# A third PSUM place for the filter outputs, gates spread at the start, and the norm's small operations moved to GpSimd

## What is computed

```python
x = x + tanh(g_xattn) * ssm(ctx, ctx, layernorm(x), ssm_kernel, D, head_dim=8)
x = x + tanh(g_ffn)   * moe(layernorm(x), Wg, W1, W3, W2, sw1, sw3, sw2)
# ssm:  kv = outer product of the 8 rows of a head of ctx with each other
#       out = causal convolution of kv with ssm_kernel[head], plus kv * D[head]
#       out = sum over i of out[i, j] * q[i], q = layernorm(x)
# moe:  softmax router, best of 8 experts, capacity 256 tokens, plus a shared expert
```

## Time and profile before

| | |
|---|---|
| median of 3 runs | 214.48 us (214.38 to 215.14) |
| the profiled execution | 214.29 us, its span 212.6 us |
| granted TensorE clock over the span | 0.991 of full speed |
| busy: PE, DVE, ACT, POOL | 198.7, 159.9, 91.9, 123.8 us |

### The profile page before, as it was taken

One profiled execution on the slowest core, in us unless ns is written; L12 is line 12 of the kernel. 1 busy time (PEld: TensorE's weight loads), 2 busy tenths in 40 slices (PEclk: granted clock), 3 DMA queues, 4 the chain that ended last, 5 costly groups with the idle time before them and its releaser, 6 DMA issues.

```text
span 212.6 us, 4239 instructions
## 1 busy us (share of the span) xinstructions
PE 198.7 (93%) x1441; PEld 184.0 (87%) x1441; DVE 159.9 (75%) x518; ACT 91.9 (43%) x182; POOL 123.8 (58%) x129
## 2 busy tenths in 40 slices
PE   5979999899999999999999998999999999999960
PEld 5957789679998989988989998999999999999950
DVE  4798788966998987589867877776856995878530
ACT  2242733193443651322348258654373445624400
POOL 4379999274648599614583253370072687677671
PEclk9999999999999999999999999999999999999996
DMA  5799993000000010010201799845537689422221
GB/s 158 245 339 359 371 396 133 0 0 3 5 0 0 0 53 17 33 54 0 92 10 50 229 357 360 298 125 138 166 106 245 187 261 329 128 78 72 67 91 49
DMA packets 21497, 29.77 MB, mean 140 GB/s; under 512 B 2834, under 2 KB 18970, under 8 KB 21476
## 3 DMA queue, kind: packets, MB, share of 16 engines
q1 hardware_dynamic: 18964, 23.24, 33.3%
q0 software_dynamic: 2304, 6.05, 8.7%
q10 hardware_dynamic: 208, 0.22, 0.4%
HBM read 21.32 MB, written 8.45 MB: 140 GB/s over the span
## 4 chain that ended last, share of the span: by engine, by line
PE 83%; DVE 4%; DMA 4%; issue 3%; ACT 2%; POOLq 1%; ACTq 0%; SPq 0%; DVEq 0%; POOL 0%
PE fb L1294 16%; PE z L1294 14%; PE z L1206 11%; PE tp L1231 10%; PE z L1203 6%; PE z L1315 6%; PE z L1329 5%; PE fb L1329 4%; DMA x_sb<-x 3%; PE fb L1315 2%; DVE terms L509 2%; PE tp L1243 2%; PE tp L1340 2%; DMA dcol<-skip_d 1%; DVE stats L923 1%
## 5 line engine op out<-in xcount | busy, mean ns | idle before, releaser
L509 DVE TENSOR_TENSOR terms<-z,qr 128x512 f32<-128x512 f32 (+2 forms) x192 | 48.9, 326 | 6.5 <-PE z L1206 6.4
L1206 PE MATMUL z<-kv,toep 128*128 128x288 f32 x128 | 41.5, 406 | 0.0
L1294 PE MATMUL fb<-xTh,wh_gu 128*128 128x256 f32 (+1 forms) x104 | 31.9, 306 | 0.2 <-issue 0.2
L490 POOL TENSOR_TENSOR kv<-ct 128x768 f32<-128x768 f32 x15 | 27.4, 1827 | 6.6 <-PE z L1206 3.3
L1203 PEld LDWEIGHTS z<-kv,toep 128*128 128x128 f32 x128 | 22.1, 190 | 9.2 <-issue 4.8
L716 POOL DMA_INDIRECT kv<-out,tok x16 | 20.4, 1273 | 16.3 <-DMA out<-x_sb 11.7
L1203 PE MATMUL z<-kv,toep 128*128 128x144 f32 x128 | 26.8, 291 | 2.8 <-DVE terms L509 1.9
L1294 PE MATMUL fb<-xTl,wh_gu 128*128 128x256 f32 (+1 forms) x104 | 29.0, 279 | 0.0
L1294 PE MATMUL fb<-xTh,wl_gu 128*128 128x256 f32 (+1 forms) x104 | 29.0, 279 | 0.0
L662 POOL TENSOR_TENSOR terms<-terms 128x512 f32<-128x512 f32 x16 | 20.2, 1281 | 14.1 <-DVE terms L509 14.0
L667 POOL DMA_INDIRECT xd_scratch<-xrow,dest x16 | 16.7, 1044 | 17.1 <-DVE xrow L1002 7.3
(11 more groups left out here) (154 smaller groups left out, 417.9 us busy)
## 6 DMA issues: line engine op xcount, KB each, us to landing
terms<-w SPq DMA_DIRECT2D x16, 352.0 KB, 4.3
ct<-ctxt SPq DMA_DIRECT2D x3, 768.0 KB, 8.8
xd_scratch<-xrow SPq DMA_DIRECT2D x4, 516.0 KB, 9.7
kv<-xd_scratch SPq DMA_DIRECT2D x8, 258.0 KB, 3.4
out<-x_sb SPq DMA_DIRECT2D x8, 256.0 KB, 2.6
terms<-w SPq DMA_DIRECT2D x8, 256.0 KB, 4.7
x_sb<-x SPq DMA_DIRECT2D x3, 512.0 KB, 6.0
toep<-kskip_scratch SPq DMA_DIRECT2D x3, 512.0 KB, 9.8
```

The source lines that it names most:

```text
L490: eng.tensor_tensor(dst, left, right, ALU.mult)
L509: return eng.tensor_tensor(view(terms, t0 + row * TROW + col, [[64, 2], *td]), view(src, zo, [[512, 2], *zd]), view(qr, q0 + qo, [[CW, 2], ...
L1206: mm = pe.matmul(z[s % 2][:, k, 0:KVH], toep[:, h, 0:P], view(kv, o, [[1, KVH]]), start=False, stop=True, skip_group_check=True)
L1294: mm = pe.matmul(bank[0:rows(blk, c), m * 256:(m + 1) * 256], wt[w % 2][:, col:col + rows(blk, c)], xt[:, place, k, first:first + 256], st ...
```

## The change

Five edits:

- PSUM: `fb` becomes one tensor `fbz` of two banks, and the filter outputs of slots 0 to 11 rotate over three places, z[0], z[1] and fbz. From slot 12 they use the two old places. A place is waited for by the last slot that used it (`z_before`).
- Gates: their two DMAs go from SP's queue to ACT's, behind the first piece of ctx. The matmul that spreads them (in slot 6 before) comes right behind `convolve(0)`. ACT copies the result to SBUF (`gate_bc`) ahead of its squares of group 0, and takes the tanh of the copy in slot 6. PE's first use of the third place (slot 2) waits for that copy.
- Norms: L928 and L929 leave DVE. POOL makes `veps` and `mneg` at the head of `scale_and_bias`, with a wait between `veps` and what follows. DVE signals POOL behind the last L926.
- ln1 of group 3: stats in slot 13 in place of 17, POOL and ACT parts in slot 14 in place of 18. Its `turn_q` stays in slot 21. The order of the norms stays.
- `router_placed` now waits for one DMA of `small_in` in place of three.

```diff
+THREE_BANKS = 12
...
+NORM_SOONER = 4
...
     if step in PREPARING:
-        g, late = divmod(s - STEPS[step], UNITS)
-        return g + 1 if late == 0 and 0 < g + 1 < NG else -1
+        sooner = NORM_SOONER if step != "turn_q" else 0
+        return next((g for g in range(1, NG) if s == UNITS * (g - 1) + STEPS[step] - (sooner if g == NG - 1 else 0)), -1)
...
+def z_place(s):
+
+    return s % 3 if s < THREE_BANKS else (s - THREE_BANKS) % 2
+
+
+def z_before(s):
+
+    return max((k for k in range(s) if z_place(k) == z_place(s)), default=-1)
...
-        fb = [ctx.enter_context(nc.psum_tensor(f"fb{i}", [P, 512], F32)) for i in range(2)]
+        fbz = ctx.enter_context(nc.psum_tensor("fbz", [P, 2, 512], F32))
+        fb = [fbz[:, i, :] for i in range(2)]
+        z_banks = [*z, fbz]
...
-            sp.dma_start(gates[:, 0:1], bass.AP(g_x.tensor, g_x.offset, [[0, 1], [1, 1]])).then_inc(small_in, 16)
-            sp.dma_start(gates[:, 1:2], bass.AP(g_f.tensor, g_f.offset, [[0, 1], [1, 1]])).then_inc(small_in, 16)
...
+                chain(pool.tensor_scalar(veps[:, :], mv[:, :, 1], EPS, None, ALU.add))
+                pool.tensor_scalar(mneg[:, :], mv[:, :, 0], -1.0, None, ALU.mult)
                 chain(pool.tensor_tensor(rstd[:, :], veps[:, :], mhalf[:, :], ALU.pow))
...
             act.dma_start(ct[:, 0, 0:4 * CW], ctxt[0, :, 0:4 * CW]).then_inc(ctx_first, 16)
+            act.dma_start(gates[:, 0:1], bass.AP(g_x.tensor, g_x.offset, [[0, 1], [1, 1]])).then_inc(gates_in, 16)
+            act.dma_start(gates[:, 1:2], bass.AP(g_f.tensor, g_f.offset, [[0, 1], [1, 1]])).then_inc(gates_in, 16)
...
             q_copy(0)
+            act.wait_ge(spread, 2)
+            act.activation(gate_bc[:, :], fb[1][:, 2:4], ACT.Copy).then_inc(gates_copied, 1)
             for c in range(1, 4):
                 squares(0, c)
...
-                    act.wait_ge(small_in, 16 * 3)
-                    act.wait_ge(spread, 2)
-                    act.activation(tg[:, :], fb[1][:, 2:4], ACT.Tanh).then_inc(tanh_done, 1)
+                    act.wait_ge(small_in, 16)
+                    act.wait_ge(gates_copied, 1)
+                    act.activation(tg[:, :], gate_bc[:, :], ACT.Tanh).then_inc(tanh_done, 1)
...
-                chain(ins)
-                dve.tensor_scalar(veps[:, :], mv[:, :, 1], EPS, None, ALU.add)
-                dve.tensor_scalar(mneg[:, :], mv[:, :, 0], -1.0, None, ALU.mult).then_inc(stats_done, 1)
+                ins.then_inc(stats_done, 1)
...
-                if s >= 2:
-                    pe.wait_ge(prods, s - 1)
+                if z_before(s) >= 0:
+                    pe.wait_ge(prods, z_before(s) + 1)
+                elif z_place(s) == 2:
+                    pe.wait_ge(gates_copied, 1)
+                zs = z_banks[z_place(s)]
...
             convolve(0)
+            pe.wait_ge(d_in, 1)
+            pe.wait_ge(gates_in, 32)
+            pe.matmul(fb[1][:, 2:4], ones[0:1, :], gates[:, :], start=True, stop=True).then_inc(spread, 1)
             for s in range(SLOTS):
                 if 1 <= s < CONV:
                     convolve(s)
-                if s == ROUTER_SLOT:
-                    pe.wait_ge(small_in, 16 * 3)
-                    pe.matmul(fb[1][:, 2:4], ones[0:1, :], gates[:, :], start=True, stop=True).then_inc(spread, 1)
```

More of the change, by code:

```diff
@@ L278, in build @@
         tg = sb("tg", [P, 2])
+        gate_bc = sb("gate_bc", [P, 2])
         ebase = sb("ebase", [P, GB, E])
@@ L333, in build @@
         small_in = sem("small_in")
+        gates_in = sem("gates_in")
+        gates_copied = sem("gates_copied")
         shared_gu_in = sem("shared_gu_in")
@@ L947, in products @@
                     dve.wait_ge(tp_ready, TP_AT[("r", before, 1)] + 1)
-                multiply(dve, s, z[s % 2]).then_inc(prods, 1)
+                multiply(dve, s, z_banks[z_place(s)]).then_inc(prods, 1)
             def first_residual(g, k):
@@ L1201, in convolve @@
                     o = (4 * g + i) % KVRING * KVQ + h % 4 * KVH
-                    pe.matmul(view(z[s % 2], k * 512 + GB, [[PL, NPL], [1, GB]]), toep[:, h, P:2 * P],
+                    pe.matmul(view(zs, k * 512 + GB, [[PL, NPL], [1, GB]]), toep[:, h, P:2 * P],
                               view(kv, o, [[PL, NPL], [1, GB]]), start=True, stop=False,
                               skip_group_check=True)
-                    mm = pe.matmul(z[s % 2][:, k, 0:KVH], toep[:, h, 0:P], view(kv, o, [[1, KVH]]),
+                    mm = pe.matmul(zs[:, k, 0:KVH], toep[:, h, 0:P], view(kv, o, [[1, KVH]]),
                                    start=False, stop=True, skip_group_check=True)
```

## The result

The changed kernel takes 215.76 us (median of 18 runs, 214.58 to 217.47) against 214.44 us for the kernel before, timed beside it on the same chip (18 runs, 213.88 to 215.14): a ratio of 1.007, interval 1.0049 to 1.0091. That is 1.3 us slower and above the predicted range. The profiled execution took 215.43 us with a span of 213.7 us, 1.1 us more than the span of before.

A forecast was written before the change was run, and what follows sets the result against it. The prediction took PE to be bound, up to `turn_xT` of group 0, by POOL's norm chain. Three times s = 0.37 us less 1.19 us of slack gave -0.08 us, so 214.4 us, range 213.2 to 215.6.

The forecast's parts named there:

- term s: Time the two small POOL operations add to each `scale_and_bias`: 0.37 us, between 0.27 and 0.65.
- What bounds the stream: Up to `turn_xT` of group 0, PE waits for ACT, which waits for POOL's `nbias`; removed DVE waits reappear there.
- Rival B: POOL isn't the chain and PE keeps the third place's gain: 2.6 us, giving 211.9 us; chance 0.07.
- The slacks: Time that absorbs POOL's delay before `turn_xT`: 0.18 us on POOL, 0.40 and 0.27 on DVE, 0.34 on ACT.
- Steps 2 to 5: From ln1 of group 2 to ACT's q copy: s added twice more, less the slacks, leaving -0.08 us.
- rival C: POOL's operations are dear in slots 2, 10 and 11: 215.2 us at s = 0.65, 216.3 at 1.0; chance 0.10.
- Step 1: `scale_and_bias(1)` has no idle time ahead, so `nbias` and `turn_q` of slot 5 come about 0.4 us later.
- The first norm: `nbias` 0.35 us later, or 0.8 if both operations wait for DVE's L490; swallowed by `turn_q` of slot 5.
- rival D: PE's 2.2 us standstill before `turn_xT` costs its clock: +1 to +1.5 us, 215.4 to 215.9 us; chance 0.06.
- Behind it each engine follows PE, and the shift goes through to the end: After `turn_xT` of group 0 at 46.6 us, PE's gain or loss there reaches the end unchanged.
- Moved norm, gates and their DMAs: ln1 of group 3 four slots sooner worth 0 to PE; gate DMAs on ACT's queue 0; gate matmul covered by a wait.

The follow-up runs named there:

- x7: The changed kernel with POOL's two small operations done twice in every norm; 219.21 us.
- x3: The changed kernel with ln1 of group 3 back in slots 17 and 18; 215.62 us, ratio 1.0090 to the kernel before.
- x4: The kernel before with only the two small norm operations moved to POOL; ratio 1.0048 to the kernel before.
- y2: The changed kernel with 16 chained memsets at the head of POOL's program; ratio 1.0044 to the kernel before.
- x5: The kernel before with only the third place and early gates, norms on DVE and in their old slots; ratio 0.9946 to the kernel before.
- x1: The changed kernel with 16 identity transposes between `turn_q` and `turn_xT` in slot 13; 214.65 us, ratio 1.0035 to the kernel before.
- y1: The changed kernel with the small operations back on DVE and 16 chained memsets heading POOL's program; 213.66 us, ratio 0.9950 to the kernel before.
- x8: The changed kernel, unchanged, timed again on another chip; 215.68 us, ratio 1.0019 to the kernel before.

## Why the prediction was wrong

The forecast was 214.4 us, range 213.2 to 215.6; it came to 215.76. Two steps of the sum failed. The term s, the price of the small operations on POOL, was set at 0.37 us and measured 0.55 to 0.70 at the three norms, which turns -0.08 us at `turn_xT` into +0.49. And the shift was to go through to the end unchanged: the tail added 0.69 us in the trace, and the clock fell in some runs. With s alone set right the sum would still lie within the range. Point by point:

- *What bounds the stream.* Right. `turn_xT` of group 0, behind ACT, behind POOL's `nbias`; the removed waits for DVE came back as waits for ACT (0.88 us at 22.68, foretold 1.2 us at 22.5; 2.39 us at 45.87, foretold 2.2). Rival B is out: with 1.9 us of waits gone the stream was no shorter.
- *The size s*: the term that was mis-sized. Foretold 0.17 + 0.07 + 0.13 = 0.37; measured 0.23 (`veps`) + 0.09 + 0.19 (until the power starts, 19.01 to 19.20) = 0.51 us; the start behind the kv work comes 0.11 later (0.08 us behind its end, where the power of before started 0.03 ahead of it), and the power lasts 1.04 in place of 1.00 us. From K to the end of `nbias` that made 0.70 us at the first norm in the stream, and it works out at 0.64 and 0.55 us at the next two: a mean of 0.63, near the upper end of the range of s, 0.65. I took one input to be a little less dear than the two of a product (0.20); the row says 0.23 for one input and a constant.
- *The slacks* were a little larger than read. Steps 2 to 5 had 0.18 + 0.27 + 0.40 + 0.34 = 1.19 us. From the trace: 0.18, then 0.48 us at DVE's second residual (L1132 to L957 took 3.47 us before, 2.99 us after), then the 0.27 of the two operations as read (from the end of the aggregate to POOL's start 0.36 us before, 0.09 after), then 0.43 us on ACT, as the q copy starts 0.10 us before xrow ends. That is 1.36, and 0.70 + 0.64 + 0.55 - 1.36 = +0.53 us, against the +0.49 measured. With the form of the sum kept and only s set right, 0.70 + 0.64 + 0.55 - 1.19 = +0.70 us, close to rival C's lower price (+0.76), it would have said 215.2 us. So C was the case for the stream, and 0.10 was too little for it. x7 confirms the slope of three: +1.78 us for another 0.5 to 0.6.
- *Step 1*: `turn_q` of slot 5 is 0.69 us later from K on, foretold 0.4. It is s again.
- *The first norm*: `nbias` ended at 9.53 us in place of 8.88, 0.65 us later, within the foretold 0.35 to 0.8, and swallowed by slot 5 as the prediction says. DVE's statistics started 0.30 us later there (4.75 in place of 4.45 us, behind a DMA), so the change itself made 0.35. `veps` on POOL took 1.18 us beside DVE's L507 (6.61 to 7.83). The Trainium skill (SBUF — State Buffer, Who interferes with whom) says that such a pair excludes each other for a whole instruction. The trace agrees: 1.18 against 0.23 us. The rule was no reason for a different time.
- *The clock*: rival D had its mechanism and its price right (+1 to +1.5 us; measured 1.5) and the chance too low. It came on top of the rest in 7 of 18 runs; it moves the median by about 215.76 - 215.35 = 0.4 us. That the median lies in the 215.4 to 215.9 us foretold for D is luck: the runs without a low clock have 215.35 us, and most of the loss is C and the tail. The prediction held its rivals to exclude each other and so had no place for C, D and more in one kernel.
- *"Behind it each engine follows PE, and the shift goes through to the end"*: wrong. This was the step that nothing was read for. The shift arrived at the last matmul (+0.59 us from K on, 0.41 in the span's own time, 204.94 to 205.35), but the tail took 0.69 us more, by its place in POOL's program. No rival had it. Any change to the number of POOL's instructions, even in idle time, could have caused it.
- *Moved norm, gates and their DMAs*: 0, right (x3; the gates' matmul stands at 13.19 us in the wait for the Toeplitz matrices).

The account: +0.49 us in the stream, 0.10 between it and the last matmul and +0.69 in the tail make the 1.28 of the traces; the clock adds 0.4 in the median. That is 1.7 against 1.3 us measured, where K is known in the profiles alone. Other kernels fit the same prices. x4: 0.50 + 0.54, a ratio of 1.0048, measured 1.0048. y2: 0.47 + 0.0 and 3 of 12 low-clock runs at 1.5 us, a mean of 0.85, 1.004, measured 1.0044. x5: -0.94, 0.9956, measured 0.9946. x3: 0.48 + 0.62 and 3 of 6 low-clock runs, 1.0087, measured 1.0090. Three don't fit, all with the long issues and all faster than the prices say. x1: 0.50 + 0.62, 1.0052, measured 1.0035 (1.0021 to 1.0050). y1: -1.11 + 0.56, 0.9974, measured 0.9950 (0.9932 to 0.9968). x8: 0.45 + 0.52 and 2 of 12 low-clock runs, 1.0057, measured 1.0019 (0.9987 to 1.0051). So the price of the stream is shown; that of the tail fits x3 and x4 and is too high for these three, and how the remaining loss splits between the tail, the clock and the timing of before stays open.

## What to carry to other kernels

Freeing a busy engine by handing its small work to one with more idle time pays only if the receiver isn't on the chain at that moment. POOL was 61% busy and idle for long stretches, but in slots 2, 10 and 11 each 0.1 us on it was 0.1 us of PE, three times over. A wait of TensorE that is harmless by itself can cost more afterwards: ask of each edit how long the longest wait becomes, beside how late the work is. And measure a part of the kernel that the edit doesn't touch, the tail here, before the sum is trusted.

## What the runs showed of the hardware

- A wait of 2.39 us of PE ahead of `turn_xT` was followed by a mean granted clock of 0.982 or less in 15 of 48 runs, 1.5 us dearer; 1.64 us or less there, in none of 153. A run's mean clock can hide a fall, so the 15 may be too few. With 3.59 us the clock was 0.87, 0.50 and 0.78 in the next three stretches of 2 us. With identity transposes in the wait none of 12 runs had a low clock (x1).
- An indirect DMA is issued by POOL in 1.0 us, but some in 1.5 to 2.4; which ones depends on the place in POOL's program. 16 more memsets, 2.5 us of idle time, moved the long ones about and changed the stretch from the last matmul to the end by 0.6 to 0.7 us, either way (y1, y2); in the medians less of it is seen. A transfer of the kind "instruction" on q14 lies within 0.6 us of the start of the first long issue in all six traces that have it, and none lies beside the same issue in the other eight. Whether it is the cause stays open.
- POOL on 128x4: 0.23 to 0.25 us for an operation with a constant, 0.20 for a product, 1.00 to 1.04 for a power; a chained wait is 0.07 to 0.09 us.
- The landing of one input DMA varied by 2.35 us between executions (10.19 to 12.54 us), and everything up to 46 us moved with it.
